# Attention scores of a routed transformer block: two passes of rounded parts in place of plain 32-bit products, and reads over two banks

## The chip, the core and the metric

The kernel runs on one core of one Trainium2 chip. The metric is the device time in microseconds (us); lower is better. The core has a matrix engine (TensorE, PE in the profile), three engines for elementwise work (VectorE or DVE, ScalarE or ACT, GpSimd or POOL) and SyncE (SP), which issues most of the DMAs. Each engine works through its own queue in order; semaphores tie the queues together.

## What is computed

Two layers over x of shape (32, 256, 256). In each, tokens go through a conditional branch and then a routed feed-forward. The change lies in the attention of the first layer:

```python
# c: output of the conditional branch of the first layer, per batch (256 tokens, 256 channels)
n = c * rsqrt(mean(c * c) + 1e-6) * attn_norm_w
q = (n @ wq.T).reshape(B, S, 16, 16)              # 16 heads of 16
k = (n @ wk.T).reshape(B, S, 4, 16)               # 4 key heads, each for 4 query heads
v = (n @ wv.T).reshape(B, S, 4, 16)
attn = einsum('bqhd,bkhd->bhqk', q, repeat(k)) / 4
attn = softmax(where(causal, attn, -inf))
h = c + einsum('bhqk,bkhd->bqhd', attn, repeat(v)).reshape(B, S, C) @ wo.T
out = h + moe(rmsnorm(h))                         # best 2 of 8 experts by gate logits
...
# layer 2: x @ W_base + low-rank part, then 16 experts that pick their 32 best tokens, and a shared expert
```

## The kernel before

The kernel has five stages, one after the other: the conditional feed-forward of the first layer (`cond_ffn_phase`), the attention (`attention_phase`), the products of the routed tokens of the first layer (still in `attention_phase`, behind its loop), the second layer's low-rank part and shared expert, and its 16 experts (`experts_phase`).

The attention stage has one loop over the 32 batches, written out in full. Each engine has its own `body(i)`, which lists its work of lap i in order; a lap works on several batches at once. In lap i, TensorE does `turned_scores` of batch i, `scores` of batch i+1, the projections of batch i+2 and the output of batches i-1 and i-2.

- Batch i+2: `front.load` brings the rows, ScalarE and GpSimd normalise them, TensorE turns them (`turn_norm`), and `keys_values` (L666) and `queries` (L688) project them with rounded high and low parts: `exact_product` sums three products of parts. Keys and values land in the bank `piece_b`, queries in `piece_a`. `keep_kv` (L678, VectorE) writes the keys to `k_t`, with a row of ones in each group of 32 rows; `keep_q` (L696, ScalarE) writes the queries to `q_t`. The 16 heads stand as 4 groups of 32 rows (a key head each); the even query heads are in the first 16 rows of a group. The odd ones come out in the last 16 rows, and `move_odd_heads` (L700, SyncE) moves them to the first 16 by 4 DMAs, one a group.
- Batch i+1: `scores` (L1708) computes 128 queries against their keys, plain 32-bit, 16 rows of a group each, in three rounds r: rounds 0 and 1 the later 128 queries against 256 keys, for two heads of each group at a time, round 2 the earlier 128 queries against 128 keys, for all four. Masks are added by small bf16 products (L1734). Each group has its own bank. The banks form a ring of six (`slot`), from which `maxima` (L1241, VectorE, one bank each) takes the negative maximum of each row. `turn_max` (L1778, TensorE) turns the maxima into rows, `keep_shift` copies them (q1: ScalarE, q0: VectorE) and `move_shift` (L933, SyncE) moves them by DMA to row 16 of each group of `q_t`. There they meet the ones of `k_t`.
- Batch i: `turned_scores` (L1738) computes the scores again the other way round, keys by queries, plain 32-bit, with 17 rows, so that the maximum is subtracted by the product itself. `exps` (L1135, ScalarE, one bank each) takes the exponentials into the weights, GpSimd cuts them to the causal half (`keep_earlier`), and `values` (L1761) multiplies them with v.

The order of TensorE's work in a lap is `turned_scores` 0, `project_out`, `turn_max` 0, `scores` 0, `turn_norm`, `values` 1, `turned_scores` 1, `turn_h`, `heads` 0, `scores` 1, `heads` 1, `keys_values`, `queries` 0, `turned_scores` 2, `prefix` and `gate`, `queries` 1, `turn_max` 1, `scores` 2, `turn_out`, `values` 0.

The order of SyncE's queue in a lap (L980) is `move_shift` of q0, the loads of c and x and the store of the sums, the load of a later batch, `move_shift` of q1 for batch i+1, `move_odd_heads` for batch i+2, and in some laps one load of zeros or of later weights. `scores` 0 of the next lap waits for the moved heads (L1714), `turned_scores` 0 and 1 for the shifts.

A wait for the ring: a round of `scores` or `turned_scores` writes banks that were read two thirds of a turn before, and `ring_free` (L1704) waits for the maxima and exponentials of these. In rounds 1 and 2 of `scores` the third and fourth group wait for one exponential each (L1726).

## Time and profile before

| | |
|---|---|
| median of 3 runs | 2114.61 us (2113.46 to 2119.59) |
| the profiled execution | 2111.37 us, its span 2109.7 us |
| TensorE busy | 2036.1 us (97%), weight loads 1752.2 us (83%) |
| VectorE busy | 1347.3 us (64%) |
| ScalarE busy | 1117.4 us (53%) |
| GpSimd busy | 963.0 us (46%) |
| maxima, L1248, 384 times | 250.0 us, 681 ns each |
| exponentials of the diagonal weights, L1139, 256 times | 138.5 us, 599 ns each |
| `scores`, L1727, 2048 instructions | 124.0 us with a part of them at work |
| `turned_scores`, L1752, 768 instructions | 112.7 us |
| moves of odd heads, L702 | 128 DMAs, 32 KB each |

How to read it: busy time is the time in which at least one instruction of the engine runs; TensorE's instructions overlap, so that a mean of one can't be multiplied by the count. What one costs is read from the starts in a timeline. SyncE's work is the issuing of DMAs; it isn't counted as busy and shows in the queue's own timeline (SPq). The granted clock is that of TensorE, 1.00 for 2.4 GHz and 0.50 for 1.2 GHz.

### The profile page before, as it was taken

To read this page: it belongs to the slowest core of one execution; us is meant where nothing else is said; L and a number is where in the kernel's file an instruction comes from. 1 tells how busy PE (TensorE), PEld (TensorE's weight loads), DVE (VectorE), ACT (ScalarE), POOL (GpSimd) and SP (SyncE) were. 2 spreads that over 40 slices of the span, in tenths; PEclk is the share of its full clock that TensorE was granted. 3 is DMA by queue.
4 is the path that set the end of the run, shared out by engine and by line. 5 is a ranking of instruction groups with operands and counts; after the bars stand their busy time and mean duration, and the time that the engine had idled before them with its cause. 6 is when DMAs were issued, how large, how long until landed. Compare 5 with 4: busy or idle time off the path is not lost. (4 is left out here: it accounts for less than half of the span.)

```text
span 2109.7 us, 50236 instructions
## 1 busy us (share of the span) xinstructions
PE 2036.1 (97%) x17544; PEld 1752.2 (83%) x17544; DVE 1347.3 (64%) x2818; ACT 1117.4 (53%) x2219; POOL 963.0 (46%) x1062
## 2 busy tenths in 40 slices
PE   7999989999999999989979999999899999999997
PEld 7999985666666666659979999999888888888886
DVE  7888954676777767765636776788654444444452
ACT  6777744666666666655543333344354444454542
POOL 0000002365565556556644444444245656565653
PEclk9999987999999999989989999999999999999998
DMA  8767711133233232229864444544344444545442
GB/s 294 264 260 267 261 59 31 62 104 96 92 108 110 87 106 96 78 92 305 300 218 144 148 151 142 175 150 151 104 96 109 95 111 95 112 96 111 96 83 30
DMA packets 134682, 289.62 MB, mean 137 GB/s; under 512 B 23026, under 2 KB 64755, under 8 KB 128243
## 3 DMA queue, kind: packets, MB, share of 16 engines
q1 hardware_dynamic: 84466, 177.25, 24.9%
q0 software_dynamic: 50048, 110.14, 20.3%
q8 instruction: 105, 1.72, 0.3%
q14 instruction: 63, 0.51, 0.1%
HBM read 187.17 MB, written 95.42 MB: 134 GB/s over the span
## 5 line engine op out<-in xcount | busy, mean ns | idle before, releaser
L1248 DVE TENSOR_REDUCE neg_max<-ring 128x2 f32<-128x512 f32 (+1 forms) x384 | 250.0, 681 | 106.4 <-PE ring L1734 106.1
L1041 POOL TENSOR_SCALAR_AFFINE_SELECT weights_diag<-weights_diag 128x512 f32<-128x512 f32 x256 | 158.3, 643 | 258.4 <-ACT weights_diag L1139 258.1
L2908 POOL DMA_INDIRECT out<-q_t,row_put x128 | 201.8, 1576 | 162.4 <-ACT q_t L2972 137.7
L3046 DVE TENSOR_TENSOR ex_hid<-ex_up_ps,gelu 128x512 f32<-128x512 f32 x128 | 86.9, 688 | 171.8 <-ACT gelu L2956 171.8
L2956 ACT ACTIVATE gelu<-ex_gate_ps 128x512 f32<-128x512 f32 x128 | 76.3, 596 | 187.3 <-PE ex_up_ps L62 187.3
L2379 POOL DMA_INDIRECT picked_rows<-results,lo_row_now x128 | 134.0, 1047 | 56.3 <-issue 29.8
L1139 ACT ACTIVATE weights_diag<-ring 128x512 f32<-128x512 f32 x256 | 138.5, 599 | 24.2 <-PE ring L1752 24.2
L60 PE MATMUL ex_down_ps<-ex_dn_lo,ex_hid_hi 128*128 128x256 f32 x512 | 145.1, 283 | 2.8 <-issue 2.8
L61 PE MATMUL ex_down_ps<-ex_dn_hi,ex_hid_lo 128*128 128x256 f32 x512 | 145.2, 284 | 0.0
L62 PE MATMUL ex_down_ps<-ex_dn_hi,ex_hid_hi 128*128 128x256 f32 x512 | 144.9, 283 | 0.0
L1049 POOL DMA_INDIRECT sorted_rows<-h_sb,row_now x128 | 126.8, 990 | 34.8 <-issue 31.3
L360 POOL DMA_DIRECT2D c<-c_sb x31 | 17.1, 552 | 273.2 <-DVE c_sb L430 273.2
L1727 PE MATMUL ring<-k_t,q_t 16*128 16x128 f32 (+1 forms) x2048 | 124.0, 356 | 9.1 <-DVE neg_max L1248 4.3
L1139 ACT ACTIVATE weights_full<-ring 128x512 f32<-128x512 f32 x128 | 66.1, 603 | 103.5 <-PE ring L1752 103.5
L1752 PE MATMUL ring<-q_t,k_t 17*128 17x512 f32 x768 | 112.7, 657 | 3.7 <-DVE neg_max L1248 3.3
L2426 ACT ACTIVATE ht_hi<-turned 128x512 fp32r<-128x512 f32 x32 | 19.2, 599 | 181.9 <-PE turned L2713 181.9
L1727 PEld LDWEIGHTS ring<-k_t,q_t 16*128 16x128 f32 x2048 | 89.4, 194 | 31.3 <-issue 23.7
L3039 DVE TENSOR_TENSOR ex_xt_lo<-ex_turned,ex_xt_hi 128x512 fp32r<-128x512 f32 x64 | 41.3, 686 | 107.2 <-ACT ex_xt_hi L2950 107.2
L2963 ACT ACTIVATE ex_hid_hi<-ex_hid 128x512 fp32r<-128x512 f32 x128 | 79.1, 628 | 41.5 <-DVE ex_hid L3046 41.5
L60 PEld LDWEIGHTS ex_down_ps<-ex_dn_lo,ex_hid_hi 128*128 128x128 f32 x512 | 97.0, 189 | 4.6 <-issue 3.3
L61 PEld LDWEIGHTS ex_down_ps<-ex_dn_hi,ex_hid_lo 128*128 128x128 f32 x512 | 97.0, 189 | 1.4
L62 PEld LDWEIGHTS ex_down_ps<-ex_dn_hi,ex_hid_hi 128*128 128x128 f32 x512 | 97.5, 190 | 0.0
(404 smaller groups left out, 7521.8 us busy)
## 6 DMA issues: line engine op xcount, KB each, us to landing
ug_raw<-in_w_ug SPq DMA_DIRECT2D x32, 1028.0 KB, 5.0
dn_raw<-in_w_dn SPq DMA_DIRECT2D x32, 640.0 KB, 5.2
q_t<-sorted_rows SPq DMA_DIRECT2D x136, 128.0 KB
moe_w<-in_expert_gu SPq DMA_DIRECT2D x16, 1024.0 KB, 4.8
results<-c0n POOLq DMA_DIRECT2D x33, 256.0 KB, 4.4
x_raw<-in_x_t SPq DMA_DIRECT2D x32, 256.0 KB, 5.1
c0n<-c SPq DMA_DIRECT2D x32, 256.0 KB, 4.3
c0r<-c SPq DMA_DIRECT2D x32, 256.0 KB
```

The costliest lines, as they stand in the source:

```text
L60: nc.tensor.matmul(out, lhs_hi, rhs_lo, start=start, stop=False)
L61: nc.tensor.matmul(out, lhs_lo, rhs_hi, start=False, stop=False)
L62: return nc.tensor.matmul(out, lhs_hi, rhs_hi, start=False, stop=stop)
L1041: nc.gpsimd.affine_select(part, part, [[0, G], [1, P]], ALU.is_ge, 0.0, base=0, channel_multiplier=-1).then_inc(kept_done, 1)
L1049: nc.gpsimd.indirect_dma_start(out=sorted_rows, out_offset=to, in_=h_sb[b[1] % 4][:, t, :], in_offset=None).then_inc(scattered[b[1] % 2], 16)
L1139: nc.scalar.activation(tile[:, g, :], slot(2 * r, g)[:], ACT.Exp).then_inc(exp_done, 1)
L1248: nc.vector.tensor_reduce(out, src, AX_X, ALU.max, negate=True).then_inc(max_done, 1)
L1727: nc.tensor.matmul(slot(2 * r + 1, g)[:, c * keys:(c + 1) * keys], q_t[n][rows, j, q * P:(q + 1) * P], k_t[n][rows, 0:keys], start=(c == 0 ...
L1752: nc.tensor.matmul(slot(2 * r, g)[:], k_t[n][rows, k * P:(k + 1) * P], q_t[n][rows, :, q * P:(q + 1) * P], start=True, stop=True).then_inc ...
L2379: nc.gpsimd.indirect_dma_start(out=picked[par][:, n, :], out_offset=None, in_=results, in_offset=bass.IndirectOffsetOnAxis(ap=row_now[par] ...
L2908: nc.gpsimd.indirect_dma_start(out=out_rows, out_offset=bass.IndirectOffsetOnAxis(ap=at, axis=0), in_=eo[c][:, n, :], in_offset=None, comp ...
L3046: nc.vector.tensor_tensor(hid[f % 2][:], up_ps[f % 2][:], gelu[f % 2][:], ALU.mult).then_inc(hid_done, 1)
```

## The change

- `q_t` and `k_t` hold rounded parts. The queries are kept as a high part (`keep_q`) and a low part (`low_q`, new, VectorE, two operations of 512 elements). The keys come out of the projection twice, once in each half of a group's 32 rows, and are kept three times: the high part with two rows of ones, and two stacks of high and low part over 32 rows, one for even and one for odd heads (`keep_k`, new, ScalarE, two operations; `keep_kv`, VectorE, two more).
- A score is then a product of the high parts over 16 rows plus one product over 32 rows, which holds both mixed terms (`scores` and `turned_scores`). All are rounded 32-bit (float32r). Before, each product was plain 32-bit.
- `move_heads` takes the place of `move_odd_heads`: 12 DMAs a batch for 4. It waits for both halves of `low_q`.
- The maxima are split in two parts (`split_max`, new), turned together, and moved to two rows by two DMAs for one (`move_shift`).
- `maxima` and `exps` read two banks by one instruction. The ring comes free in pairs.
- In `body`, `queries` 1 moves ahead of `turned_scores` 2, `keep_k` and `keep_q` move ahead of the exponentials of round 2 on ScalarE, and `keep_shift` between the two.
- There are three buffers of `q_t` and `k_t` in place of four, two of them in the memory of the shared expert's weights; the last stage writes its rows from other buffers.

```diff
     def keep_kv(self, dve, b, k_t, v):
...
-        self.nc.vector.tensor_scalar(k_t[:], self.piece_b[:, 0:S], self.at.one_rows[:], None, ALU.add)
...
+        rows, high = self.at.k_rows, k_t[:, 1, :].bitcast(F32)
+        self.nc.vector.scalar_tensor_tensor(out=k_t[:, 2, :], in0=high, scalar=rows[:, 3:4], in1=self.piece_b[:, 0:S], op0=ALU.mult, op1=ALU.add).then_inc(self.k_odd_done, 1)
+        dve.wait_ge(self.k_odd_done, b + 1)
+        self.nc.vector.scalar_tensor_tensor(out=k_t[:, 1, :], in0=high, scalar=rows[:, 2:3], in1=self.piece_b[:, 0:S], op0=ALU.mult, op1=ALU.add).then_inc(self.b_free, 1)
...
+    def keep_k(self, act, b, k_t):
+
+        act.wait_ge(self.kv_done, b + 1)
+        rows = self.at.k_rows
+        self.nc.scalar.activation(k_t[:, 1, :], self.piece_b[:, 0:S], ACT.Copy).then_inc(self.k_hi_done, 1)
+        self.nc.scalar.activation(k_t[:, 0, :], self.piece_b[:, 0:S], ACT.Identity, bias=rows[:, 0:1], scale=rows[:, 1:2]).then_inc(self.k_hi_done, 1)
...
-    def move_odd_heads(self, sp, b, q_t):
+    def low_q(self, dve, b, q_t, c):
+        dve.wait_ge(self.q_hi_done, b + 1)
+        whole = self.piece_a[:, c * S:(c + 1) * S].unsqueeze(1).broadcast_to([P, 2, S])
+        high = q_t[:, 0, 2 * c, :].bitcast(F32).unsqueeze(1).broadcast_to([P, 2, S])
+        self.nc.vector.tensor_tensor(q_t[:, 1, 2 * c:2 * c + 2, :], whole, high, ALU.subtract).then_inc(self.a_free if c == QB - 1 else self.q_lo_done, 1)
+
+    def move_heads(self, sp, q_t):
+
+        q_t = q_t.bitcast(F32)
         for g in range(NKV):
-            sp.dma_start(q_t[32 * g:32 * g + HD, 1:G:2, :], q_t[32 * g + HD:32 * g + HALF, 0:G:2, :]).then_inc(self.odd_heads_in[b % 2], 16)
+            even, odd = slice(32 * g, 32 * g + HD), slice(32 * g + HD, 32 * g + HALF)
+            for rest in range(2):
+                sp.dma_start(q_t[even, rest, 1:G:2, :], q_t[odd, 0, 0:G:2, :]).then_inc(self.heads_in, 16)
+            sp.dma_start(q_t[odd, 1, 0:G:2, :], q_t[even, 0, 0:G:2, :]).then_inc(self.heads_in, 16)
...
             def move_shift(b, q):
                 sp.wait_ge(b_free, per_b(f"shift_q{q}", later(b, -q)) + 1)
-                sp.dma_start(q_t[b[1] % 4][HD:P:32, :, q * P:(q + 1) * P], shift[q][:]).then_inc(shift_in[q], 16)
+                for h in range(2):
+                    sp.dma_start(q_t[b[1] % 3].bitcast(F32)[HD + h:P:32, 0, :, q * P:(q + 1) * P], shift[q][h * NH:(h + 1) * NH, :].bitcast(F32)).then_inc(shift_in[q], 16)
...
+            def move_heads(i):
+                sp.wait_ge(front.q_lo_done, i[1] + 3)
                 sp.wait_ge(a_free, per_a("q", i) + 1)
-                front.move_odd_heads(sp, i[1] + 2, q_t[(i[1] + 2) % 4])
+                front.move_heads(sp, q_t[(i[1] + 2) % 3])
...
-            def exps(b, r, groups):
+            def exps(b, r, h):
                 tile = (weights_diag1[b[1] % 2], weights_diag0, weights_full)[r]
...
+                act.wait_ge(turned_done[2 * h], times(3, b, r + 1))
+                act.wait_ge(turned_done[2 * h + 1], times(3, b, r + 1))
+                nc.scalar.activation(tile[:, 2 * h:2 * h + 2, :], slot_pair(2 * r, h)[:], ACT.Exp).then_inc(exp_done, 2)
...
+            def split_max(b, q):
+                dve.wait_ge(max_done, times(12, b, 8 if q else 12))
+                whole = neg_max[q][:].rearrange("p g j -> p (g j)")
+                nc.vector.tensor_copy(max_parts[q][:, 0, :], whole).then_inc(max_hi_done, 1)
+                dve.wait_ge(max_hi_done, times(2, b, 1 if q else 2))
+                nc.vector.tensor_tensor(max_parts[q][:, 1, :], whole, max_parts[q][:, 0, :].bitcast(F32), ALU.subtract).then_inc(max_parts_done[q], 1)
...
                     until(pe, b_free, per_b("kv", later(i, -1)) + 1)
-                    pe.wait_ge(odd_heads_in[(i[1] + 1) % 2], 16 * NKV * ((i[1] + 1) // 2 + 1))
+                    pe.wait_ge(front.heads_in, 48 * NKV * (i[1] + 2))
...
                 for c, j in enumerate(heads_):
-                    for g in range(NKV):
-                        rows = slice(32 * g, 32 * g + HD)
-                        if r and c == 0 and g >= 2:
-                            until(pe, exp_done, no_more_than(times(12, i, 4 * r + g - 1), 12 * B))
-                        nc.tensor.matmul(slot(2 * r + 1, g)[:, c * keys:(c + 1) * keys], q_t[n][rows, j, q * P:(q + 1) * P], k_t[n][rows, 0:keys],
-                                         start=(c == 0), stop=False)
+                    for rest in range(2):
+                        for g in range(NKV):
+                            rows = slice(32 * g, 32 * g + (HALF if rest else HD))
+                            if r and c == 0 and not rest and g == 2:
+                                until(pe, exp_done, no_more_than(times(12, i, 4 * r + 2), 12 * B))
+                            nc.tensor.matmul(slot(2 * r + 1, g)[:, c * keys:(c + 1) * keys], q_t[n][rows, rest, j, q * P:(q + 1) * P],
+                                             k_t[n][rows, 1 + j % 2 if rest else 0, 0:keys], start=(c == 0 and not rest), stop=False)
...
                 for g in range(NKV):
-                    rows = slice(32 * g, 32 * g + HD + 1)
-                    nc.tensor.matmul(slot(2 * r, g)[:], k_t[n][rows, k * P:(k + 1) * P], q_t[n][rows, :, q * P:(q + 1) * P],
-                                     start=True, stop=True).then_inc(turned_done[g], 1)
+                    rows = slice(32 * g, 32 * g + HD + 2)
+                    nc.tensor.matmul(slot(2 * r, g), k_t[n][rows, 0, keys], q_t[n][rows, 0, :, toks], start=True, stop=False)
+                for odd in range(2):
+                    for g in range(NKV):
+                        rows = slice(32 * g, 32 * g + HALF)
+                        out = slot(2 * r, g).rearrange("p (j s) -> p j s", j=G)[:, odd:G:2, :]
+                        last = nc.tensor.matmul(out, k_t[n][rows, 1 + odd, keys], q_t[n][rows, 1, odd:G:2, toks], start=False, stop=(odd == 1))
+                        if odd:
+                            last.then_inc(turned_done[g], 1)
...
                     keys_values(i)
                     queries(i, 0)
+                    queries(i, 1)
                 if has:
                     turned_scores(i, 2)
...
-                if has_next:
-                    queries(i, 1)
```

## Rows read from the trace of the kernel before

**Rows 1.** Busy time by stretch: us, PE, PEld, DVE, ACT, POOL, clock, DMA, GB/s

```profile
300.00:345.00 45.00, 38.12 (x317) 26.80 (x308) 18.51 (x36) 14.28 (x33) 6.22 (x10) 0.56 0.09 25
...
400.00:500.00 100.00, 100.00 (x1221) 67.34 (x1214) 70.52 (x206) 63.90 (x152) 53.15 (x69) 1.00 0.28 88
```

**Rows 2.** Timeline of PE, one lap: start, us, engine, line, operation, out<-in, shapes, count

```profile
599.77 1.15 PE L1727 MATMUL ring<-k_t,q_t 16*128 16x256 f32 x16
600.74 0.46 PE L1734 MATMUL ring<-maskb,at_placeb 32*128 32x256 bf16 x16
601.12 0.66 PE L1793 MATMUL piece_b<-at_ident,normed 128*128 128x128 f32 x4
601.71 1.06 PE L1773 MATMUL piece_a<-weights_diag,v 128*32 128x512 f32 x8
602.59 1.04 PE L1773 MATMUL piece_a<-weights_full,v 128*32 128x512 f32 x8
603.57 1.14 PE L1752 MATMUL ring<-q_t,k_t 17*128 17x512 f32 x8
604.64 0.66 PE L1793 MATMUL piece_b<-at_ident,h_sb 128*128 128x128 f32 x4
...
605.66 1.32 PE L1727 MATMUL ring<-k_t,q_t 16*128 16x256 f32 x16
...
610.09 1.14 PE L1752 MATMUL ring<-q_t,k_t 17*128 17x512 f32 x8
...
613.06 0.27 PE L1782 MATMUL piece_b<-at_ident,neg_max 128*16 128x128 f32 x1
613.26 1.17 PE L1727 MATMUL ring<-k_t,q_t 16*128 16x128 f32 x32
...
619.28 1.15 PE L1727 MATMUL ring<-k_t,q_t 16*128 16x256 f32 x16
```

**Rows 3.** Timeline of SyncE's own queue in the same lap

```profile
613.66 0.58 SPq L935 DMA_DIRECT2D q_t<-shift  x1
614.28 2.60 SPq L702 DMA_DIRECT2D q_t<-q_t  x4
616.92 0.58 SPq L954 DMA_DIRECT2D moe_w<-in_moe_w  x1
```

**Rows 4.** Line L702: issues (ns, minimum, median, maximum) and time to landing

```profile
L702 SPq DMA_DIRECT2D q_t<-q_t x128: 585/610/1417, 282.4 to 907.8; - x128
...
DMA to landing us min/median/max: 1.9/2.0/3.1
```

**Rows 5.** Timeline of ACT in the same lap

```profile
611.25 2.07 ACT L1139 ACTIVATE weights_full<-ring 128x512 f32<-128x512 f32 x4 [3.04 <-PE ring L1752]
613.37 0.27 ACT L1159 ACTIVATE shift<-piece_b 16x128 f32<-16x128 f32 x1
```

**Rows 6.** Timeline of PE, two neighbouring products of rounded parts (`keys_values`)

```profile
607.93 0.28 PE L62 MATMUL piece_b<-nt_hi,wqk_hi 128*128 128x256 f32 x1
608.05 0.28 PE L60 MATMUL piece_b<-nt_lo,wqk_hi 128*128 128x256 f32 x1
```

**Rows 7.** Timeline of PE behind idle times, late and early in the stage

```profile
919.73 0.79 PE L1787 MATMUL piece_a<-at_ident,ot_sb 128*128 128x128 f32 x4 [1.76 <-DVE o L1264]
922.15 2.09 PE L1752 MATMUL ring<-q_t,k_t 17*128 17x512 f32 x8 [1.62 <-DVE neg_max L1248]
...
347.75 1.11 PE L1793 MATMUL piece_b<-at_ident,normed 128*128 128x128 f32 x4
348.79 1.68 PE L1773 MATMUL piece_a<-weights_diag,v 128*32 128x512 f32 x8
350.30 1.03 PE L1773 MATMUL piece_a<-weights_full,v 128*32 128x512 f32 x8
```

**Rows 8.** Groups of VectorE by shape, 345 to 960 us: busy, mean ns, idle before

```profile
L1248 DVE TENSOR_REDUCE neg_max<-ring 128x2 f32<-128x512 f32 x240 | 157.1, 681 | 16.0 <-PE ring L1734 15.7
...
L685 DVE TENSOR_REDUCE v<-piece_b 128x64 f32<-128x128 f32 x58 | 13.8, 278 | 0.0
```

More of the change, by code:

```diff
@@ L246, in _ @@
             load_down(PAIRS - 1, 1)
+            sp.wait_ge(front.q_lo_done, 1)
             sp.wait_ge(front.a_free, 1)
-            front.move_odd_heads(sp, 0, front.q_t[0])
+            front.move_heads(sp, front.q_t[:])
             sp.wait_ge(c0_done, B)
@@ L350, in body @@
                 elif is_at(j, par, 30):
-                    front.keep_q(act, 0, front.q_t[0])
+                    front.keep_k(act, 0, front.k_t)
+                    front.keep_q(act, 0, front.q_t)
             rolled(act, first, body, lambda: None, WRITTEN_OUT)
@@ L485, in body @@
                 elif is_at(j, par, 30):
-                    front.keep_kv(dve, 0, front.k_t[0], front.v[0])
+                    front.keep_kv(dve, 0, front.k_t, front.v)
+                    for c in range(QB):
+                        front.low_q(dve, 0, front.q_t, c)
             def last():
@@ L996, in body @@
                 if exists(later(i, 2)):
[L997 removed]
+                    move_heads(i)
                 if 0 <= i[1] - 4 < EM:
@@ L1576, in body @@
                 if has_next:
-                    front.keep_kv(dve, i[1] + 2, k_t[(i[1] + 2) % 4], v[(i[1] + 2) % 4])
+                    front.keep_kv(dve, i[1] + 2, k_t[(i[1] + 2) % 3], v[(i[1] + 2) % 3])
                 if has_scores:
-                    maxima(s, 1, 2)
-                    maxima(s, 1, 3)
+                    split_max(s, 1)
+                if has_next:
+                    front.low_q(dve, i[1] + 2, q_t[(i[1] + 2) % 3], 0)
+                    front.low_q(dve, i[1] + 2, q_t[(i[1] + 2) % 3], 1)
                 if picks:
@@ L1588, in body @@
                     maxima(s, 2, 0)
-                    maxima(s, 2, 1)
                 if picks:
@@ L1596, in body @@
                 if has_scores:
-                    maxima(s, 2, 2)
+                    maxima(s, 2, 1)
+                    split_max(s, 0)
                 if picks:
                     scaled_odds(m_pick)
-                if has_scores:
-                    maxima(s, 2, 3)
                 if picks:
@@ L3221, in lay_out @@
     k_rows = np.zeros((1, NKV, HALF, D), np.float32)
-    k_rows[0, :, 0:HD] = a[F0 + "wk"].reshape(NKV, HD, D)
+    for n in range(2):
+        k_rows[0, :, n * HD:(n + 1) * HD] = a[F0 + "wk"].reshape(NKV, HD, D)
+    row = np.arange(P) % HALF
     d = {
```

148 lines of the change are left out of this document (76 added, 72 removed).

## The prediction

> **What bounds the kernel now.** I read the table of stretches first. In the attention stage (about 318 to 945 us of the span) one lap over the batches is the unit, and TensorE is busy for the whole of a stretch such as 400 to 500 us, at the full granted clock (2.4 GHz), while VectorE is busy for 70.5% of it and ScalarE for 63.9% [rows 1]. So TensorE sets the pace. Then the timeline of TensorE over one lap: the three groups of score products `scores` (start 599.77, 605.66, 613.26) and of `turned_scores` (603.57 and 610.09 are two of three), with the next lap's first `scores` at 619.28. The lap is 619.28 - 599.77 = 19.51 us [rows 2], and no row in it shows an idle time. Third, the queue of SyncE, because the change moves more by DMA: in the same lap it issues one move of the shift at 613.66, then the four moves of the odd heads from 614.28 to 616.88, then the next item at 616.92 [rows 3]. A queue issues one after the other: four in 2.60 us, 0.66 us from one start to the next once the gap of 0.04 is counted. One such move lands 2.0 us after its issue starts [rows 4]. The last of the four starts at 614.28 + 3 x 0.66 = 616.26 and lands at 618.3; the first `scores` of the next lap, which waits for it, starts at 619.28. The spare is 1.0 us. That is the number on which the forecast turns.
>
> **TensorE's own part.** Plain 32-bit products take two instructions for each product: 16 instructions for the 8 products of `scores` round 0, from 599.77 to 600.74, 0.97 us; 8 instructions for the 4 products of a `turned_scores`, from 603.57 to 604.64, 1.07 us [rows 2]. Four row groups of the array work side by side here. After the change round 0 has again 16 instructions, 4 for each row group, 256 columns, in rounded parts. The nearest row of rounded parts is the key and query projection, 256 columns over all 128 rows: 0.12 us from start to start [rows 6]. Side by side, 4 x 0.12 = 0.48 us (one after the other 16 x 0.12 = 1.9 us, the other end). I take 0.49, since the rounding changes the operands and not the row groups: saves 0.48, twice a lap (rounds 0 and 1). Round 2 has 32 instructions of 128 columns before (1.00 us less the start of the masks) and after; each needs its own weights, and 128 columns of weights do not get shorter. I take no gain (0 to 0.14). A `turned_scores` has one product of 512 columns and two of 256 for each row group, as long as four of 256: 0.50 us, saves 0.57, three times. Sum for TensorE: 2 x 0.48 + 3 x 0.57 = 2.67 us a lap, 19.51 to 16.8. The transposes of maxima in two parts (32 columns of weights in place of 16) I leave at their 0.20 [rows 2]; the mask products are unchanged.
>
> **What VectorE and ScalarE pay.** A maximum over one bank takes 681 ns and a reduction of 128 elements 278 [rows 8], so 403/384 = 1.05 ns an element and 0.144 fixed: over two banks 1.22 us, six times 1.22 for twelve times 0.68, saves 0.86. `low_q` adds 2 x 0.68, the keys 3 operations for 1 (about +0.4), `split_max` four small ones at about 0.15: together +2.4. Net +1.5 us a lap on some 13.8 (70.5% of 19.51), 15.3: below the new lap in every case below, though 91% of a lap of 16.8. ScalarE saves about 0.17 on each of six exponentials (four of 512 take 2.07 us [rows 5], so about 0.52 each in a run and some 1.0 for a pair) and pays two copies of 256 in `keep_k`: about level. One wait grows: the third row group of `scores` round 1 needs the banks of the first pair of exponentials, which now comes free when both are done, about 1.05 + 0.8 us after the end of `turned_scores` (the emptying of the values goes first on ScalarE), while TensorE comes to it after turn_h and heads, 1.02 us [rows 2], plus some 0.4. I count 0.45 us of stall, between 0 and 0.9. The extra waits in `split_max` and `keep_kv` have the queries, a `turned_scores` and the gate as cover, some 3 us between the key projection and `turn_max` 1; VectorE needs some 2 us of it, and if it is later than that, the delay goes straight onto the lap.
>
> **What SyncE pays, and who waits.** `move_heads` issues 12 moves for 4, and each of the two `move_shift` 2 for 1; the shapes of the heads' moves are those of [rows 4] (16 partitions, two runs of 1 KB). In the queue, `move_shift` for q1 stands ahead of `move_heads`, and so the heads still leave only after `turn_max` 1, though the queries are now ready earlier. The loop of one lap is then:
> - first `scores` to `turn_max` 1: 613.06 - 599.77 = 13.29 before [rows 2]; less 0.48 + 0.57 + 0.48 + 0.57, plus the stall of 0.45: 11.64
> - `turn_max` to the issue of the shift: 613.66 - 613.06 = 0.60 [rows 2, 3], of which ScalarE's copy at 613.37 is part [rows 5]; 0.65, since that copy now stands right behind a double exponential
> - two shift issues at 0.62: 1.24
> - eleven issues up to the start of the twelfth: 11 x 0.66 = 7.26
> - landing: 2.0
> Sum 22.8 us, against 19.5 before and 17.3 (16.84 + 0.45) that TensorE would need. So TensorE stands idle for 5.5 us in front of the first `scores` of each lap. Queued behind this wait on TensorE are the masks, the transposes of the norms and the values; ScalarE and VectorE run dry. Queued behind the 12 moves on SyncE are the parts of the expert weights and the next lap's shift for q0, which needs to land only for `turned_scores` 1, about 3.3 us after the first `scores`: it is issued 1.9 us after the heads and holds nothing up.
>
> **The clock.** An idle time of this length every lap is new. In the trace, two idle times of 1.76 and 1.62 us within 4 us were enough: the `turned_scores` behind them took 2.09 in place of 1.14 us, the 1.2 GHz level [rows 2, 7], and the mean granted clock of 300 to 345 us was 0.56 [rows 1]. It comes back in the dense products of the values: transposes at 347.75 took 1.04 to the next start where 0.59 is usual (601.12 to 601.71), the first values 1.51 where 0.88 is usual (601.71 to 602.59), the second ones are at full speed again [rows 2, 7]. So a fall in each idle time costs 0.45 for the transposes, 0.63 for the values, about 0.5 for the score products and 0.4 for the masks, all on the loop: 2.0 us a lap (0 where the clock holds, 2.9 where all values are slow). The Trainium skill (TensorE: Matmul & The Clock Gate, "HAM oscillation — how this bites in real kernels") says that waits between bursts in a loop make the clock fall anew in each turn; these rows agree. I take 22.8 + 2.0 = 24.8 us.
>
> **The sum.** 31 laps wait for moved heads; the first is slow already before the change (the clock at half), so 30 count: 30 x (24.8 - 19.5) = 159 us. The stages before and after keep their times: the heads of batch 0 leave 5 us later under 15 us of cover, and the experts merely write from other buffers. The profiled run took 2111.4 us (its span 2109.7, 1.7 around it) and lies 3.2 us under the median of 2114.6, within the spread of the runs. 2111.4 + 159 = 2270 us.
>
> **The rivals.**
> - Clock holds. Same queue, 22.8 us a lap: 30 x 3.3 = 99, 2210 us. For it: one idle time of 1.7 us alone need not pull the clock down. Against: 5.5 us is over three times that.
> - Faster: the queue does not bind. If the issues ran ahead of the moves, or cost less when many stand in a row, the lap would be TensorE's 17.3 us: 30 x -2.2 = -66, 2045 us, VectorE 88% busy and next in line. It decides at the issue time x for which 11.64 + 0.65 + 1.24 + 11x + 2.0 = 19.5, x = 0.36 us. Every one of the 128 moves took at least 0.585 [rows 4], and the four that stand in a row did not get cheaper. The Trainium skill (DMA: Bandwidth & Descriptors, "Anatomy of one DMA — SWDGE (gpsimd) path") has a dispatch of about 50 ns and says that many descriptors can be emitted before their cost shows; it describes the other kind of queue, and by it this rival would be the outcome.
> - The rounded products don't share the array's row groups. Round 0 and 1 then take 1.9 us (+0.9), a `turned_scores` 1.9 (+0.8): the loop grows by 3.4 over 13.29, 16.7 + 11.15 = 27.8 us a lap, 30 x 8.3 = 249, 2360 us. Nothing in the trace shows such products in row groups either way.
> - The clock stays down for whole laps. The 11.64 us take some 10 more: over 33 us a lap, some 2520 us. Against: where values follow, the clock came back.
>
> **How the numbers follow.** Slow queue with falling clock 0.55 (2225 to 2330); slow queue with the clock held 0.20 (2165 to 2225); row groups apart 0.08; clock down for good 0.06; faster 0.08; the gain and the wait cancelling, within 0.3%, 0.03. The low end is the held clock with no ring stall and issues of 0.61 us: 22.8 - 0.45 - 0.55 = 21.8, 30 x 2.3 = 69, some 2180, and 10 under it for the rest; the high end takes in the third rival. Range 2170 to 2365. Slower by over 0.3% 0.89, within 0.3% (some 6 us, about what this measurement can tell) 0.03, faster 0.08.
>
> **What would show it.** Right: `move_heads` twelve in a row for 7.9 us in SyncE's queue, each lap; the first `scores` of a lap with an idle time of about 5 us, released by a DMA; `scores` round 0 at about 0.5 and `turned_scores` at 0.5 us; a mean granted clock of the stage well under 1; VectorE near 60%. Wrong: a lap under 19.5 us; moves that leave before the shift; issues under 0.4 us; or TensorE busy throughout.

## The result, and the profile of the changed kernel

The changed kernel takes 2305.2 us (median of 4 runs, 2303.0 to 2310.6), the kernel before took 2116.2 us beside it (4 runs, 2113.5 to 2119.6). The ratio is 1.090, with a 95% interval from 1.0885 to 1.0913. The profiled execution of the changed kernel has a span of 2301.4 us against 2109.7: 191.7 us more.

The stretch from 400 to 500 us, with the columns of [rows 1]:

```profile
400.00:500.00 100.00, 82.27 (x958) 57.08 (x956) 62.29 (x152) 50.79 (x101) 37.45 (x50) 0.85 0.24 72
```

Where [rows 1] has TensorE busy throughout at full clock, it is now busy for 82% at a granted clock of 0.85, and VectorE and ScalarE are less busy than before. Nothing is full: the engines wait for each other, or for a queue.

TensorE over one lap, beside [rows 2] (first `scores` 612.39 and 639.59, so 27.20 us; the mean lap from 500 to 900 us is 26.2):

```profile
612.39 0.75 PE L1771 MATMUL ring<-k_t,q_t 16*128 16x256 f32 x16 [2.82 <-DMA q_t<-q_t]
612.95 0.48 PE L1778 MATMUL ring<-maskb,at_placeb 32*128 32x256 bf16 x16
613.37 0.83 PE L1844 MATMUL piece_b<-at_ident,normed 128*128 128x128 f32 x4
614.13 1.93 PE L1824 MATMUL piece_a<-weights_diag,v 128*32 128x512 f32 x8
615.83 1.68 PE L1824 MATMUL piece_a<-weights_full,v 128*32 128x512 f32 x8
617.45 0.51 PE L1797 MATMUL ring<-sh_gu_lo,sh_gu_hi 18*128 18x512 f32 x4
617.78 0.41 PE L1802 MATMUL ring<-sh_gu_lo,sh_gu_hi 32*128 32x256 f32 x8
618.13 0.66 PE L1844 MATMUL piece_b<-at_ident,h_sb 128*128 128x128 f32 x4
...
627.50 0.40 PE L1833 MATMUL piece_b<-at_ident,max_parts 128*32 128x128 f32 x1 [1.42 <-DVE logits L1386]
627.82 1.97 PE L1771 MATMUL ring<-k_t,q_t 16*128 16x128 f32 x32
629.59 1.29 PE L1778 MATMUL ring<-maskb,at_placeb 32*128 32x512 bf16 x16
...
639.59 0.63 PE L1771 MATMUL ring<-sh_gu_hi,q_t 16*128 16x256 f32 x12 [3.19 <-DMA q_t<-q_t]
```

A wait stands in brackets. There are two in each lap: for the moved heads ahead of the first `scores` (2.82, then 3.19 us), and, not forecast, 1.42 us ahead of `turn_max` 1 for VectorE's `logits`. Behind both, in this lap, rows run at the half clock: values 1.70 us to the next start where [rows 2] has 0.88, the third `scores` 1.77 where it has 1.00. Behind the wait for the heads that isn't so in every lap: in 5 of the 16 laps that start between 500 and 900 us the values there take their full-clock 1.06 us. The mean granted clock of those laps is 0.91 from the first `scores` to `turn_max` 1 and 0.65 from there to the `turn_max` 0 that follows. The products themselves are shorter, as forecast: a `turned_scores` is 0.68 us (617.45 to 618.13) where [rows 2] has 1.07.

SyncE's queue, beside [rows 3], and one of the two lines of `move_heads` (the other has nearly the same times), beside [rows 4]:

```profile
628.22 1.12 SPq L971 DMA_DIRECT2D q_t<-shift  x2
629.45 1.32 SPq L729 DMA_DIRECT2D q_t<-q_t  x2
...
634.62 1.54 SPq L730 DMA_DIRECT2D q_t<-q_t  x1
...
637.48 0.59 SPq L730 DMA_DIRECT2D q_t<-q_t  x1
```

```profile
L730 SPq DMA_DIRECT2D q_t<-q_t x88: 585/592/1541, 288.4 to 1101.0; - x88
...
  PE ring L1771: 91.5, 31
...
DMA to landing us min/median/max: 1.9/2.0/3.3
```

Twelve moves leave between 629.45 and 638.07. The last starts at 637.48, and the first `scores` at 639.59, 2.1 us later: TensorE starts on the landing. It waited so 31 times, 91.5 us in all.

VectorE between the key projection and `turn_max` 1, and GpSimd in the same microseconds:

```profile
624.48 0.48 DVE L703 SCALAR_TENSOR_TENSOR sh_gu_hi<-sh_gu_hi,k_rows,piece_b 128x256 fp32r<-128x256 f32 x1
624.88 1.06 DVE L1291 CAST max_parts<-neg_max 128x16 fp32r<-128x16 f32 x1
625.97 0.17 DVE L1293 TENSOR_TENSOR max_parts<-neg_max,max_parts 128x16 fp32r<-128x16 f32 x1
626.06 1.28 DVE L721 TENSOR_TENSOR q_t<-piece_a,q_t 128x512 fp32r<-128x512 f32 x2
627.26 0.18 DVE L1386 TENSOR_REDUCE logits<-piece_b 128x16 f32<-128x32 f32 x1
```

```profile
624.62 1.28 POOL L1091 TENSOR_TENSOR x_sb<-x_sb,h_sb 128x512 f32<-128x512 f32 x1
```

This is the second wait. `turn_max` 1 needs the bank that `keep_logits` empties, and `keep_logits` stands behind both `low_q` (1.28 us) and behind `split_max`, whose copy of 16 elements takes 1.06 us here and 0.17 elsewhere. It ends as GpSimd's addition ends (625.90).

### The profile page after: what moved, and what is told of

Its sections match the earlier page's. It is cut to its first block and busy times, and to the rows that moved or that the text cites. A ratio compares the mean times of both kernels' runs of the same rounds, so it can differ in the third digit from the quotient of the medians.

```text
span 2301.4 us, 51673 instructions
## 1 busy us (share of the span) xinstructions
PE 2090.1 (91%) x17928; PEld 1800.1 (78%) x17928; DVE 1429.2 (62%) x2850; ACT 1138.0 (49%) x2091; POOL 964.1 (42%) x1060
## 3 DMA queue, kind: packets, MB, share of 16 engines
q8 instruction: 108, 1.77, 0.3%
## 5 line engine op out<-in xcount | busy, mean ns | idle before, releaser
L1286 DVE TENSOR_REDUCE neg_max<-ring 128x4 f32<-128x1024 f32 (+1 forms) x192 | 233.3, 1217 | 208.8 <-PE ring L1778 208.7
L2958 POOL DMA_INDIRECT out<-c0n,row_put x64 | 101.0, 1578 | 115.5 <-ACT c0n L3022 105.4
L1176 ACT ACTIVATE weights_diag<-ring 128x1024 f32<-128x1024 f32 x128 | 130.3, 1022 | 11.5 <-PE ring L1802 8.6
L1824 PE MATMUL piece_a<-weights_diag,v 128*32 128x512 f32 x512 | 107.9, 931 | 3.4 <-DVE h_sb L1333 2.9
L1184 ACT ACTIVATE ot_sb<-piece_a 128x512 f32<-128x512 f32 x64 | 38.3, 598 | 115.7 <-PE piece_a L1824 115.7
L3101 DVE TENSOR_TENSOR ex_hid_lo<-ex_hid,ex_hid_hi 128x512 fp32r<-128x512 f32 x128 | 86.8, 688 | 7.4 <-ACT ex_hid_hi L3013 2.2
L60 PE MATMUL ps_up<-x_lo,ug_hi 128*128 128x256 f32 x256 | 73.3, 286 | 11.6 <-DVE ug_lo L440 11.1
```

The costliest lines, as they stand in the source:

```text
L60: nc.tensor.matmul(out, lhs_hi, rhs_lo, start=start, stop=False)
L1176: nc.scalar.activation(tile[:, 2 * h:2 * h + 2, :], slot_pair(2 * r, h)[:], ACT.Exp).then_inc(exp_done, 2)
L1286: nc.vector.tensor_reduce(out, src, AX_X, ALU.max, negate=True).then_inc(max_done, 2)
L1824: last = nc.tensor.matmul(piece_a[32 * g:32 * g + 32, :], v[b[1] % 3][:, k, g, :], tile[:, g, :], start=(c == 0), stop=(c == len(parts) - 1))
L2958: nc.gpsimd.indirect_dma_start(out=out_rows, out_offset=bass.IndirectOffsetOnAxis(ap=at, axis=0), in_=eo[c][n], in_offset=None, compute_op ...
L3101: nc.vector.tensor_tensor(hid_lo[c][:, f, :], hid[f % 2][:], hid_hi[c][:, f, :].bitcast(F32), ALU.subtract).then_inc(hid_lo_done, 1)
```

## The experiments

For each kernel I took the laps whose first `scores` start between 500 and 900 us (15 to 21 laps each) from TensorE's timeline, and the clock from the table of stretches. Means of the one profiled execution of each, in us (that of all_three was its fastest, 2177.9 us against a median of 2188.6):

| kernel | lap | first `scores` to `turn_max` 1 | of it, wait for `logits` | `turn_max` 1 to next first `scores` | of it, wait for heads | clock |
|---|---|---|---|---|---|---|
| before | 19.4 | 13.2 | 0 | 6.2 | 0 | 1.00 |
| after | 26.2 | 14.8 | 1.5 | 11.4 | 2.7 | 0.84 |
| before_plus8 | 27.0 | 16.2 | 0 | 10.8 | 4.5 | 0.88 |
| filler | 25.4 | 17.6 (filling and wait for heads in it) | 1.0 | 7.8 | 0.6 | 0.90 |
| four_moves | 23.4 | 15.3 | 1.1 | 8.2 | 0 | 0.86 |
| pool_moves | 23.9 | 15.3 | 1.3 | 8.5 | 0.2 | 0.83 |
| logits_first | 26.4 | 14.9 | 0.3 | 11.5 | 3.9 | 0.83 |
| cast_reduce | 26.3 | 14.9 | 1.2 | 11.4 | 3.3 | 0.85 |
| four_early | 22.2 | 14.3 | 0.3 | 7.9 | 0 | 0.87 |
| all_three | 21.8 | 13.5 | 0.4 | 8.3 | 1.3 | 0.93 |
| four_late_turned | 21.2 | 14.4 (filling in it) | 0.3 | 6.9 | 0 | 0.95 |
| all_late_turned | 23.3 | 15.1 (filling in it) | 0.3 | 8.2 | 1.6 | 0.93 |
| two_banks | 19.8 | 13.4 | 0 | 6.4 | 0 | 0.99 |

**The queue alone: before_plus8.** The kernel before, its products untouched, with eight more moves in SyncE's queue, of the same shape.

```diff
                 front.move_odd_heads(sp, i[1] + 2, q_t[(i[1] + 2) % 4])
...
+                for g in range(NKV):
...
+                    sp.dma_start(spare[even, 0], q[odd, 0:G:2, :]).then_inc(odd_heads_in[i[1] % 2], 16)
+                    sp.dma_start(spare[odd, 0], q[even, 0:G:2, :]).then_inc(odd_heads_in[i[1] % 2], 16)
```

> The kernel before with nothing changed but the queue: eight more moves a lap on SyncE's queue behind the four of the odd heads, same shape (16 rows, two runs of 1 KB), into memory that is not read until it is loaded anew; the first score products of a lap wait for all twelve. Theory (the queue of SyncE sets the lap): the spare of 1.0 us is used up and 8 x 0.64 = 5.1 us are added, so at least 4.1 us a lap of idle time in front of the first score products, plus up to 2 us for the lower clock behind it: lap 23.5 to 25.6 us for 19.5, 30 laps, 120 to 185 us more, about 2236 to 2300 us. Rival (TensorE or VectorE slowed by the new products, not the queue): the moves are hidden, under 20 us more, about 2116 to 2135 us.

Measured: 2335.8 us, ratio 1.102 (1.1002 to 1.1042). The first `scores` of a lap:

```profile
701.89 2.09 PE L1732 MATMUL ring<-k_t,q_t 16*128 16x256 f32 x16 [4.12 <-DMA sh_gu_lo<-q_t]
703.73 0.78 PE L1739 MATMUL ring<-maskb,at_placeb 32*128 32x256 bf16 x16
```

Eight moves alone cost more than the whole change does, and more than the 2236 to 2300 us expected. The wait of 4.1 us is where it was forecast. The lap is longer than expected because the clock costs 3.0 us of it (16.2 against 13.2), not 2: plain 32-bit products have the more to lose at half clock (1.84 us to the next start where [rows 2] has 0.97).

**Without eight of the moves: four_moves.**

```diff
-            for rest in range(2):
-                sp.dma_start(q_t[even, rest, 1:G:2, :], q_t[odd, 0, 0:G:2, :]).then_inc(self.heads_in, 16)
-            sp.dma_start(q_t[odd, 1, 0:G:2, :], q_t[even, 0, 0:G:2, :]).then_inc(self.heads_in, 16)
+            sp.dma_start(q_t[even, 0, 1:G:2, :], q_t[odd, 0, 0:G:2, :]).then_inc(self.heads_in, 16)
```

> The changed kernel with eight of the twelve moves left out, and the wait for the moved heads cut to match: the mixed terms of the scores are then computed from rows that were never moved, so the scores are not those of the reference; every other instruction stays. Theory (queue): the wait in front of the first score products goes, 5.1 us a lap with the clock's part behind it; what is left of it is the later turning of the maxima, so a lap of about 18.5 to 20 us, 2060 to 2120 us in all. Rival (the maxima that are turned late and VectorE's part set the lap, and the moves only fill a time that is idle anyway): the lap falls by under 2 us, 2245 us or more.

Measured: 2209.5 us, ratio 1.043 (1.040 to 1.047): 96 us less than the changed kernel, but some 90 above the kernel before, and as much above the 2060 to 2120 us expected; the rival (2245 us or more) missed too. The wait for the heads is gone and the lap is 23.4 us all the same. A lap early in the stage shows what the rest is:

```profile
362.60 0.75 PE L1769 MATMUL ring<-k_t,q_t 16*128 16x256 f32 x16
...
375.17 0.28 PE L1831 MATMUL piece_b<-at_ident,max_parts 128*32 128x128 f32 x1 [0.53 <-DVE logits L1384]
...
381.16 0.75 PE L1769 MATMUL ring<-sh_gu_hi,q_t 16*128 16x256 f32 x16
```

With a wait of 0.53 us and the clock at one, the lap is 18.56 us. Later laps wait up to 1.4 us for `logits` and run the third `scores`, the masks and the values behind it at half clock. So there is a second cost. In the changed kernel the wait itself is on the loop, and the slow rows behind it run beside the queue's issues, which take longer.

**The wait filled: filler.** Twelve dense products ahead of the wait for the heads, results overwritten.

```diff
+                    for _ in range(12):
+                        nc.tensor.matmul(slot(1, 0), at.wqk_hi[:, 0, 0, :], nt_hi[:].rearrange("p k s -> p (k s)"), start=True, stop=True)
                     pe.wait_ge(front.heads_in, 48 * NKV * (i[1] + 2))
```

> The changed kernel with twelve dense products (128 rows, 512 columns, into a bank that the first score products overwrite) in front of TensorE's wait for the moved heads. They fill 12 x 0.22 = 2.6 us of an idle time of 2.0 to 3.2 us and change nothing else. Theory (the clock falls in the idle time and the products behind it pay): the masks, transposes and values behind the wait run at 2.4 GHz, 1.5 to 2.5 us a lap less, 45 to 75 us less in all, 2230 to 2260 us. Rival (the clock's part is small, or it falls all the same in the part of the idle time that is left): within 10 us of the changed kernel, or some us slower, 2295 to 2320 us.

Measured: 2285.7 us, ratio 1.078 (1.0755 to 1.080): 20 us less, where about 60 were expected from the clock; the result lies between the two expectations. The idle time ahead of the first `scores` is filled but for 0.6 us on average. From the first `scores` to `turn_max` 1 the granted clock is now 0.99 (0.91 in the changed kernel) and the stretch, without the filling, is 13.9 us for 14.8. Of these 0.85 us, 0.5 are a shorter wait for `logits`. Behind `turn_max` 1 the clock is still only 0.72: that part of its fall follows the wait for `logits`, which stays, and the queue takes its 11.4 us beside it.

**Eight moves from another queue: pool_moves.** Same work, the moves of the low parts issued by GpSimd.

```diff
-                front.move_heads(sp, q_t[(i[1] + 2) % 3])
+                front.move_heads(sp, q_t[(i[1] + 2) % 3], (0, ))
...
+                if exists(later(i, 2)):
+                    pool.wait_ge(front.q_lo_done, i[1] + 3)
+                    pool.wait_ge(a_free, per_a("q", i) + 1)
+                    front.move_heads(pool, q_t[(i[1] + 2) % 3], (1, 2), front.more_heads_in)
```

> The changed kernel with eight of the twelve moves issued from GpSimd's queue, at the end of its lap where it waits some 10 us for exponentials, and four from SyncE's. Theory (what counts is that one queue issues twelve in a row behind the shift): SyncE's part is 2.6 us, GpSimd's 8 x 0.6 to 1.1 us = 5 to 9 us but starts 2 us earlier, since it does not stand behind the shift; the heads land 1 to 4 us earlier, a lap of 21 to 24 us for 26.0, 60 to 150 us less in all, 2155 to 2245 us. If GpSimd's issues cost over 1.2 us each, the gain is gone. Rival (the moves themselves are slow to land when twelve are under way, whichever queue issues them): within 15 us of the changed kernel.

Measured: 2220.8 us, ratio 1.048 (1.046 to 1.049), 84 us less and inside what was expected. Both queues now issue side by side:

```profile
654.35 4.12 POOL L731 DMA_DIRECT2D q_t<-q_t  x8 [2.07 <-DVE q_t L722]
```

```profile
654.70 1.11 SPq L972 DMA_DIRECT2D q_t<-shift  x2
655.92 2.58 SPq L731 DMA_DIRECT2D q_t<-q_t  x4
```

It computes all that the changed kernel does, so for these 84 us the place in SyncE's queue, not the data moved, was the cost.

**The second wait, by order and by operation: logits_first, cast_reduce.**

```diff
-                if has_next:
-                    front.low_q(dve, i[1] + 2, q_t[(i[1] + 2) % 3], 0)
-                    front.low_q(dve, i[1] + 2, q_t[(i[1] + 2) % 3], 1)
                 if picks:
                     advance_rows(i)
                 if has_h:
                     keep_logits(i)
+                if has_next:
+                    front.low_q(dve, i[1] + 2, q_t[(i[1] + 2) % 3], 0)
+                    front.low_q(dve, i[1] + 2, q_t[(i[1] + 2) % 3], 1)
```

> The changed kernel with one thing moved: on VectorE the low parts of the queries are made behind the logits, not ahead of them (the logits hold the bank in which the maxima are turned). In the changed kernel TensorE waits 1.3 to 1.9 us for the logits in front of the second turning of the maxima, and that lies on the loop. Theory (the loop is 15.1 us up to that turning, then SyncE's queue): two operations of 0.64 leave it, up to 1.2 us a lap, 30 to 40 us less in all, about 2265 to 2275 us; not more, since SyncE's twelve issues stay. Rival (the loop is SyncE's queue alone and TensorE's waits inside it cost nothing): within 7 us of the changed kernel.

```diff
-                nc.vector.tensor_copy(max_parts[q][:, 0, :], whole).then_inc(max_hi_done, 1)
+                nc.vector.tensor_reduce(max_parts[q][:, 0, :], whole.unsqueeze(2), AX_X, ALU.max).then_inc(max_hi_done, 1)
```

> The changed kernel with the copy of 16 maxima a row into the rounded high part written as a reduction over one element in place of a copy (same values). In 25 of 31 laps that copy takes 1.0 to 1.7 us in place of 0.17, and ends when an addition over two buffers on GpSimd ends. Theory (a copy from memory to memory can't run beside GpSimd's addition, a reduction can): it takes 0.17 to 0.2 us in all laps, the loop is 0.9 us shorter in 25 of them, 15 to 25 us less in all, about 2280 to 2290 us. Rival (any VectorE operation on memory is held up there): no change, within 7 us.

Measured: 2311.5 us, ratio 1.091 (1.086 to 1.095), and 2317.7 us, 1.094 (1.090 to 1.099). Neither gains, though logits_first cuts the wait for `logits` from 1.5 to 0.3 us. logits_first lies in the band of its rival (within 7 us of the changed kernel); cast_reduce, expected 15 to 25 us faster, is 12 slower, with intervals that overlap. The table says where the wait went. From `turn_max` 1 to `turn_max` 0 logits_first takes 7.4 us at a clock of 0.78, where the changed kernel takes 8.4 at 0.65, but the next first `scores` waits for the queue, which started with `turn_max` 1 and takes its 11.4 us in any case: the wait for the heads grows from 2.7 to 3.9 us. Behind this longer wait TensorE runs slower, 14.5 us without the waits (14.9 less 0.3) where the changed kernel has 13.3 (14.8 less 1.5), its clock 0.83 where that has 0.91, and that stretch is on the loop. The 1.2 us were paid back in clock. cast_reduce shows that the held copy is only the first in line:

```profile
736.02 0.16 DVE L1291 TENSOR_REDUCE max_parts<-neg_max 128x16 fp32r<-128x16 f32 x1
736.22 1.22 DVE L1293 TENSOR_TENSOR max_parts<-neg_max,max_parts 128x16 fp32r<-128x16 f32 x1
```

```profile
736.12 1.27 POOL L1091 TENSOR_TENSOR x_sb<-x_sb,h_sb 128x512 f32<-128x512 f32 x1
```

As a reduction the same 16 elements pass in 0.16 us beside GpSimd, and the subtraction behind it is held in its place until GpSimd's addition ends. The Trainium skill (SBUF — State Buffer, "Who interferes with whom") says that copies and casts can contend with GpSimd for a shared port pair, held for a whole instruction, that `tensor_tensor` with both inputs in SBUF contends with GpSimd's reads, and that a reduction on this chip never contends; the copy's 1.06 us, the subtraction's 1.22 and the reduction's 0.16 agree.

**Both costs taken away: four_early, all_three.** They put the last two edits on top of four_moves and of pool_moves.

> The run with four of the twelve moves (mixed terms computed from rows that were never moved, so the scores are not those of the reference), and both edits on VectorE on top: the logits ahead of the low parts, the copy as a reduction. In the run with four moves the lap was 23.7 us, with a wait of 1.4 us for the logits, behind which everything ran at half the clock (2.7 us more). Theory (that wait is what lowers the clock): it falls under 0.3 us, the clock stays at 2.4 GHz, a lap of 17.5 to 19 us and 2035 to 2085 us in all; the laps 2 to 4 of that run already took 18.6 to 20.1. Rival (TensorE's new products leave it too idle for the high clock whatever VectorE does): the granted clock stays near 0.85 and the lap over 21 us, 2160 us or more.

> The changed kernel, complete, with all three mends: eight of the twelve moves from GpSimd's queue, logits ahead of the low parts, the copy as a reduction. Theory: SyncE issues 2 + 4 moves in 3.8 us, GpSimd 8 in 4.1 us from the moment that the low parts are done; neither the moves nor VectorE hold up TensorE, lap 17.5 to 19.5 us at the full clock, 2040 to 2110 us in all, so at or under the kernel before. Rival (one of the waits comes back in another place and lowers the clock): lap 21 to 24 us, 2150 to 2220 us.

Measured: 2177.8 us, ratio 1.028 (1.025 to 1.031), and 2188.6 us, 1.034 (1.031 to 1.037): each 32 us less than without the two edits, which gained nothing while SyncE's queue bound. Both are still slower than the kernel before. They missed by 90 and 80 us and lie in the bands of their rivals, "too idle for the high clock whatever VectorE does" and "one of the waits comes back in another place"; the trace shows where the new idle time is. In four_early a third wait stands open:

```profile
644.07 0.50 PE L1795 MATMUL ring<-q_t,k_t 18*128 18x512 f32 x4
644.40 0.42 PE L1800 MATMUL ring<-q_t,k_t 32*128 32x256 f32 x8
...
645.24 0.60 PE L1836 MATMUL piece_a<-at_ident,ot_sb 128*128 128x128 f32 x4
645.77 0.39 PE L1769 MATMUL ring<-sh_gu_hi,q_t 16*128 16x256 f32 x2
647.37 0.75 PE L1769 MATMUL ring<-sh_gu_hi,q_t 16*128 16x256 f32 x14 [1.21 <-ACT weights_diag L1174]
```

```profile
644.27 0.60 ACT L1182 ACTIVATE ot_sb<-piece_a 128x512 f32<-128x512 f32 x1 [1.36 <-PE piece_a L1822]
646.29 1.02 ACT L1174 ACTIVATE weights_diag<-ring 128x1024 f32<-128x1024 f32 x1 [1.42 <-PE ring L1800]
```

The second `scores` waits for the exponentials that free its banks, and these start 2.22 us behind the first product of the second `turned_scores`, though the record of those products ends at 644.82. In 22 laps between 420 and 911 us that product came 1.9 us behind the start of the second of its shift's two issues (2.5 behind the first), and 1.9 us is the least that a move of the heads took to land; the exponential came 1.6 to 2.3 us behind the product. Three laps before 410 us came equally close and were not late (0.88 us). In the kernel before it is 1.16 us in nearly every lap. Over all ten kernels with the new products, from 330 us on, it is never over 1.3 us where the product came 3.6 us or more behind the first issue (191 laps).

Closeness alone is not enough, and GpSimd's queue shows what else is there, in the same lap of four_early:

```profile
643.25 0.98 POOL L1084 DMA_INDIRECT sorted_rows<-h_sb,row_now  x1 [0.16 <-issue]
644.54 0.96 POOL L1084 DMA_INDIRECT sorted_rows<-h_sb,row_now  x1 [0.31 <-issue]
```

These are its two indirect transfers of routed rows: one running as the product starts at 644.07, one behind. Of the 87 laps in which the product came under 2.7 us behind the first issue (four_moves, pool_moves, four_early, all_three), 75 have the first begun ahead of that start and the second ending behind it, and there the exponential comes 1.2 to 2.3 us behind the product. The other 12 have neither begun (8 laps ahead of the first such transfer, 4 in which both come later) and show 0.86 to 0.88. The kernel before has the same transfers beside its product, 2.3 to 2.9 us behind its issue, and is not late.

**The third wait: four_late_turned, all_late_turned.** Six dense products ahead of the second `turned_scores`, results overwritten, in four_early and in all_three.

```diff
+                if r == 1:
+                    const = at.wqk_hi[:].rearrange("p k c s -> p (k c s)")
+                    for _ in range(6):
+                        nc.tensor.matmul(slot(2, 0), const[:, 0:P], const[:, 0:512], start=True, stop=True)
```

> As four_early (four of the twelve moves, so the scores of odd heads lack their low parts, as there), with six dense products of 512 columns, 1.3 us in all, put ahead of the second turned scores of each lap; their results are overwritten. Theory (these turned scores signal their end 0.7 to 1.4 us late only where their first product starts 2.5 us behind the issue of their shift, and the wait of 1.2 us ahead of the second scores follows from that): the first product comes 3.7 us or more behind the issue, the exponentials start 0.9 to 1.1 us behind it, the wait is gone, the filling takes its place and the clock stands at one for more of the time: 2120 to 2165 us. Rival (the late signal belongs to the products themselves or to the load on the DMA engines): it stays and the filling comes on top, 2200 to 2230 us.

> As all_three (twelve moves, eight of them from GpSimd's queue, the logits ahead of the low parts, the copy as a maximum), with the same six products ahead of the second turned scores. Theory: with the wait filled and the clock at one, as in the stretch from 800 to 900 us of all_three whose laps took 20.4 us, laps of 20.5 to 21.5 us: 2135 to 2170 us. Rival (the late signal stays, or GpSimd's eight moves set the lap once TensorE is quicker): 2190 to 2235 us.

Measured: 2161.3 us, ratio 1.018 (1.015 to 1.021), and 2209.0 us, 1.042 (1.038 to 1.046). In four_late_turned, inside its expected band, the third wait is gone from all laps but the first two, the clock is 0.95, and against four_early 16 us are gained (21 by the ratios), although a filling of 30 x 1.56 = 47 us stands in the lap. A lap of it at full clock:

```profile
596.40 0.77 PE L1769 MATMUL ring<-sh_gu_hi,sh_gu_lo 16*128 16x256 f32 x16
596.99 0.47 PE L1776 MATMUL ring<-maskb,at_placeb 32*128 32x256 bf16 x16
598.15 0.66 PE L1846 MATMUL piece_b<-at_ident,normed 128*128 128x128 f32 x4 [0.69 <-DVE shift L1295]
...
600.61 1.63 PE L1796 MATMUL ring<-wqk_hi 128*128 128x512 f32 x6
602.17 0.50 PE L1799 MATMUL ring<-q_t,sh_gu_hi 18*128 18x512 f32 x4
...
609.75 0.28 PE L734 MATMUL piece_b<-gate,at_ht_hi 128*128 128x16 f32 x1 [0.18 <-issue]
...
611.09 0.28 PE L1835 MATMUL piece_b<-at_ident,max_parts 128*32 128x128 f32 x1 [0.28 <-DVE logits L1384]
...
617.08 0.63 PE L1769 MATMUL ring<-k_t,q_t 16*128 16x256 f32 x12
```

The lap is 20.68 us; less the filling (1.56) and the three waits (1.15) it is 17.97 against 19.51 [rows 2]. That is an estimate, from one lap, of what the shorter products are worth with nothing in their way: 1.5 us a lap, 46 us in all. all_late_turned missed, in the band of its rival; there too the third wait is gone. With twelve moves the heads still set the lap there (wait 1.3 us in all_three, 1.6 here; the second stretch of the lap 8.3 and 8.2 us), and the filling stands in the stretch ahead of `turn_max` 1, which is on that loop: it came on top.

**The other part alone: two_banks.** The kernel before with exponentials and maxima over two banks.

```diff
-                nc.scalar.activation(tile[:, g, :], slot(2 * r, g)[:], ACT.Exp).then_inc(exp_done, 1)
+                nc.scalar.activation(tile[:, 2 * h:2 * h + 2, :], slot_pair(2 * r, h)[:], ACT.Exp).then_inc(exp_done, 2)
```

> The kernel before, with the other part of the change alone: exponentials and maxima over two banks, the scores still plain 32-bit products and four moves a lap. Theory (the score products, their moves and their parts carry the loss): four exponentials of 0.52 us become two of 1.02 us, four maxima two of 1.22 us, the first exponential of the second turned scores still starts about 1.16 us behind their first product and ends as before when the second scores come to their third bank; TensorE stays at full clock and 100% busy: within 5 us of the kernel before. Rival (a pair of banks comes free later, and the second scores wait for it): 0.5 us a lap and a clock below one, 15 to 50 us slower.

Measured: 2130.1 us, ratio 1.0048 (1.0034 to 1.0061), between the two expectations: some 10 us slower, with TensorE's record busy throughout, most laps longer by some 0.2 us, and one of 22.9 us (843.02 to 865.92) with part of it at half clock. The part gains nothing where TensorE is the bound, though it takes VectorE from 71% to 66% busy. It is a small part of the 190 us.

## Why the prediction was right, and where it was off

The forecast was slower, at 2270 us with a range of 2170 to 2365; the result is 2305. The mechanism named as the likeliest held, on its own rows. It is not the whole loss, though: with the queue relieved, four_moves and pool_moves get back 96 and 84 of the 189 us. And the nearness of the sum owes something to luck, since terms that were off in both directions cancel in the first half of the loop.

- **The queue binds: right, on the number.** The second half of the loop (`turn_max` 1 to the shift 0.65, two shift issues 1.24, eleven issues 7.26, landing 2.0) was to take 11.15 us and took 11.4 on average. In the lap shown: 0.72, 1.23, 8.03 and 2.11; one issue of 1.54 us makes up the 0.8 by which the third term is over. before_plus8 shows it without any other part of the change, pool_moves by taking it away.
- **The first half of the loop: off by 1.15 us, and that is nearly the whole miss.** 11.64 + 2.0 = 13.64 was forecast and 14.79 measured; 1.15 + 0.2 over 30 laps are 41 us, the result was 35 above. The work in it was off in both directions: 0.7 us less gained by the products than forecast, against 0.45 for a stall that did not come and 0.6 less for the clock. What is left is the wait of 1.5 us. The step that failed is the cover for `split_max` and `keep_kv`, "some 3 us", of which VectorE "needs some 2 us". It took no account of `keep_logits`, behind both `low_q`, as the step that frees the bank of `turn_max` 1, nor of the copy held by GpSimd. The sentence had the consequence right (straight onto the lap), not the size: 1.5 us, not nothing.
- **The products' gain: too large.** Forecast 2.67 us a lap. Measured from start to start in the full-clock lap of four_late_turned: first `scores` 0.59 for 0.97, second 0.74 for 0.97, third 0.95 for 1.00, three `turned_scores` of 0.68 for 1.07: 1.8 us, of which 1.5 reach a whole lap. The estimate of 0.12 us [rows 6] for a rounded product in each of four row groups was the term at fault; the groups do work side by side, as taken: a round takes 0.59 to 0.74 us, where 16 products in turn would take the prediction's 1.9.
- **The clock: right in kind, its share smaller.** 2.0 us were added for it on the loop. The work of the first half took 13.28 us where 13.29 - 1.4 of gain would be 11.9, so 1.4 us, by difference; a clock of 0.91 over 14.8 us leaves 2.7 us at the half clock, which can cost 1.3. Filling the idle time gave back less, 0.85 us, and only some 0.4 of it outside the wait for `logits`. Behind `turn_max` 1 it took another 2.8 us (8.4 from one `turn_max` to the other, 6.0 before, 0.4 of it saved), but that stretch lies beside the queue. The Trainium skill (TensorE: Matmul & The Clock Gate, "HAM oscillation — how this bites in real kernels") tells of waits for DMA of some 3 to 5 us that make the clock fall in every turn of a loop. Here mean waits of 2.7 us for a DMA and 1.5 for another engine were followed by such falls, the first in 11 of 16 laps.
- **TensorE's idle time: 5.5 us forecast ahead of the first `scores`, 2.7 found.** The other 2.8 are those slow products behind the unforeseen wait: busy in the record, and idle in effect.
- **The stall of 0.45 us at the second `scores`** is absent from the changed kernel, where the queue leaves its exponentials time. It appears when the queue is relieved, at 0.2 to 1.3 us.
- **The rival "the queue does not bind"** was put at 2045 us. No run came near: once the queue was out of the way, the wait for `logits`, the late exponentials and the clock took its place, and the full gain of 46 us would only reach some 2065. Its condition, issues under 0.36 us, failed at once (585 ns at the least, over 384 moves). GpSimd's queue takes 0.52 us for each move (4.12 / 8), so the dispatch of some 50 ns that the Trainium skill gives for that path (DMA: Bandwidth & Descriptors, "Anatomy of one DMA — SWDGE (gpsimd) path") is not what a move costs its queue; the measurement decides.
- **VectorE** was to be near 60% busy, and was at 60 to 64%; the reduction over two banks took 1.217 us as worked out from [rows 8].

What stays open: why the exponentials start late when the second `turned_scores` comes right upon the landing of its shift. That the filling cures it is shown; the filling moves the product away from the shift's issue and from GpSimd's indirect transfers at once, and no run parts the two. Nor is it shown whether the products or only their signals are late. For the signals speaks that VectorE's reciprocal, which waits for later products (L1836, 0.6 us of work), starts 0.11 us behind the exponential. The laps of two_banks and of the two kernels with everything relieved still hold small losses that I did not take apart; the complete kernel at its best, all_three, is 3.4% slower than the kernel before.

## What to carry to other kernels

When a change splits operands to save time on the bound engine, count the transfers that carry the parts, issue by issue, along the queue that closes the loop, and compare that loop with the lap before pricing anything else. Then list, for each bank that the bound engine takes, the last operation that frees it and all that stands ahead of that operation; a wait there can be paid again in the clock. And when a wait is removed while another loop binds, expect nothing: logits_first and cast_reduce gained nothing alone and 32 us once the queue was relieved.

## What the runs showed that was not expected

- A VectorE copy of 16 elements takes 0.17 us alone and 1.06 beside GpSimd's addition of 512 elements; a reduction of the same elements 0.16 us, a subtraction behind it 1.22.
- A move of 16 partitions with two runs of 1 KB costs 0.59 us of issue on SyncE's queue, 0.64 from start to start, and now and then 1.2 to 1.8; on GpSimd's queue 0.52.
- An exponential over two banks takes 1.02 us, as long as two over one bank (2.07 for four [rows 5]).
- In four_early the granted clock stayed at full speed from 640 to 654 us, with an idle time of 1.21 us at 646, and fell at 654, where an idle time of 0.28 ended: the stretches of 654 to 656 us have 0.75 and 656 to 660 0.50.
